# Second layer's slab built by DMAs inside SBUF instead of through a padded copy in DRAM

## The reference

```python
x = conv_same(x, w_init, b_init)                # 1x1: the "image"
offsets = conv_same(xi, w_off[g], b_off[g])     # 3x3, two numbers for each of 9 taps
sampled = sample_with_offsets(xi, offsets, K)   # bilinear, coordinates clipped to the image
h = depthwise_same(sampled, w_dw[g], b_dw[g])
outs.append(conv_same(h, w_pw[g], b_pw[g]))
```

## Time and profile before

| | |
|---|---|
| time, median of 3 runs | 294.44 us (291.98 to 295.67) |
| span of the profiled execution | 295.1 us |
| busy: PE / DVE / POOL / ACT | 79% / 66% / 47% / 19% |
| DMA | 5759 packets, 9.37 MB |

### The profile page before, as it was taken

How to read it: one execution, slowest core, us unless ns; L and a number is a source line. 1 busy time by engine, 2 the same in 40 slices (tenths; PEclk the granted TensorE clock), 3 DMA queues, 4 the chain that set the end, 5 groups by cost and what they waited for, 6 DMA issues and landing times.

```text
span 295.1 us, 2939 instructions
## 1 busy us (share of the span) xinstructions
PE 234.4 (79%) x908; PEld 134.6 (46%) x910; DVE 196.2 (66%) x476; ACT 57.0 (19%) x94; POOL 140.1 (47%) x196
## 2 busy tenths in 40 slices
PE   0959298988988789978883586889899788899990
PEld 0725096763336642224531142457578746343430
DVE  7767779979875387573309859998977144326286
ACT  1411924210001164513111000010101301310100
POOL 5300009786951509713404929999996010000560
PEclk9997969999996579999995769999999997799997
DMA  3529970000000000000166000000000000000000
GB/s 114 160 50 187 203 196 0 0 0 3 1 1 0 0 1 3 0 0 0 26 154 125 0 1 0 0 1 3 0 0 0 2 0 0 1 2 0 0 18 18
DMA packets 5759, 9.37 MB, mean 32 GB/s; under 512 B 2390, under 2 KB 2926, under 8 KB 5742
## 3 DMA queue, kind: packets, MB, share of 16 engines
q1 hardware_dynamic: 5742, 9.18, 13.3%
HBM read 7.48 MB, written 1.69 MB: 31 GB/s over the span
## 4 chain that ended last, share of the span: by engine, by line
PE 40%; DVE 30%; POOL 15%; issue 6%; ACT 5%; DMA 1%; DVEq 1%; POOLq 0%; ACTq 0%
POOL ring L265 12%; PE ps L1011 5%; PE ps L906 5%; PE ps L746 4%; PE ps L764 3%; DVE ps L1176 3%; PE ps L876 3%; DVE big L279 3%; PE ps L932 2%; DVE cm L1123 2%; DVE xn L1079 2%; PE ps L699 2%; PE ps L813 2%; DVE ring L287 2%; PE ps L727 2%
## 5 line engine op out<-in xcount | busy, mean ns | idle before, releaser
L265 POOL TENSOR_TENSOR ring<-big 128x384 f32<-128x384 f32 x72 | 59.2, 861 | 9.4 <-PE ps L906 4.6
L297 POOL TENSOR_TENSOR big<-big 128x512 f32<-128x512 f32 x30 | 32.0, 1095 | 38.6 <-ACT big L621 32.9
L906 PE MATMUL ps<-ring,ident 128*128 128x384 f32 x100 | 38.0, 523 | 10.2 <-POOL ring L265 5.7
L746 PE MATMUL ps<-ring,ident 128*128 128x192 f32 x126 | 26.4, 362 | 8.6 <-DVE ring L287 8.4
L1484 DVE TENSOR_TENSOR ps<-ps,ring 128x384 f32<-128x384 f32 x46 | 25.8, 562 | 9.6 <-PE ps L906 8.4
L906 PEld LDWEIGHTS ps<-ring,ident 128*128 128x128 f32 x100 | 19.1, 202 | 26.3 <-DVE ring L265 7.2
L746 PEld LDWEIGHTS ps<-ring,ident 128*128 128x128 f32 x126 | 22.6, 208 | 12.8 <-DVE ring L287 12.8
L433 POOL TENSOR_TENSOR rstd<-veps,mhalf 128x4 f32<-128x4 f32 x8 | 8.3, 1032 | 39.3 <-DVE veps L1075 39.2
L691 PE MATMUL ps<-zero,ident 128*128 128x512 f32 x34 | 22.7, 815 | 1.6 <-DVE big L1402 1.6
L554 POOL TENSOR_TENSOR big<-big 128x256 f32<-128x256 f32 (+1 forms) x12 | 7.6, 635 | 34.4 <-DVE big L1562 33.7
L265 DVE TENSOR_TENSOR ring<-big,ps 128x384 f32<-128x384 f32 x36 | 19.5, 546 | 0.1
(11 more groups left out here) (270 smaller groups left out, 397.5 us busy)
## 6 DMA issues: line engine op xcount, KB each, us to landing
big<-pad SPq DMA_DIRECT2D x8, 392.0 KB, 9.5
big<-pad SPq DMA_DIRECT2D x8, 240.0 KB, 5.5
w<-in_w_dram SPq DMA_DIRECT2D x2, 512.0 KB
w<-in_w_dram SPq DMA_DIRECT2D x2, 256.0 KB
pad<-img SPq DMA_DIRECT2D x8, 64.0 KB, 2.1
pad<-zero SPq DMA_DIRECT2D x1, 484.0 KB, 3.9
pad<-zero SPq DMA_DIRECT2D x1, 400.0 KB, 4.5
x<-in_x_dram SPq DMA_DIRECT2D x1, 256.0 KB, 2.6
```

The costliest lines, as they stand in the source:

```text
L265: return eng.tensor_tensor(V(ring, 0, slot * SP, [[1, P], [NJ * C, 3], [C1, NJ * G1], [1, C1]]), bigv((py + dy) * SLAB1 + (dx + j0) * C, [ ...
L297: return eng.tensor_tensor(dst, bigv(wy * SLAB0 + wx * C, [C0, J * G0], [1, C0]), table, ALU.mult)
L746: return mm(bank(px + dx, 0, P, [1, 3 * J * G0], off=dy * J * G0), ident[:, :], ring[:, slot + 3 * px * J * G0:slot + 3 * (px + 1) * J * G ...
L906: mm(bank(1 + i % 2, 0, P, [1, SP]), ident[:, :], ring[:, slot * SP:slot * SP + SP], start=(n == 0), stop=(n == len(srcs) - 1)).then_inc(s ...
```

## The change

The padded copy `pad1` goes, with its zero store at the start, its four stores and the eight slab loads. In their place:

- POOL clears the whole slab in `big` (3840 floats a partition) with one memset between `inv_std(5)` and `inv_std(6)`, once the semaphore `y0_ps` tells that PE has read what lies there (the hidden values of the experts).
- ACT copies the image from PSUM straight into the middle row of the slab instead of into `img`.
- SP issues two DMAs of 64 partitions x 512 bytes for the halo pixels, waits for both (`halo1`), and then four DMAs that copy the middle row (768 floats) of all partitions but the first or last few into the rows above (`slab1_above`) and below (`slab1_below`).
- POOL waits for the rows above ahead of its first product and for the rows below ahead of the second item. DVE waits for both at the place of the old wait.

```diff
-        pad0, pad1 = scratch("pad0", R0), scratch("pad1", R1)
+        pad0 = scratch("pad0", R0)
...
+            def window_rows():
+
+                mid = R1 * SLAB1
+                sp.wait_ge(sem("halo_zero"), 1)
+                sp.wait_ge(sem("img1"), 1)
+                for h, to, at in ((0, (R1 + HC) * C, R1 * C), (1, 0, HC * C)):
+                    sp.dma_start(V(big, h, mid + to, [[2, P // 2], [1, R1 * C]]),
+                                 V(big, 1 - h, mid + at, [[2, P // 2], [1, R1 * C]])).then_inc(sem("halo1"), 16)
+                sp.wait_ge(sem("halo1"), 32)
+                for wy, arrived in ((1, "slab1_above"), (0, "slab1_above"), (3, "slab1_below"), (4, "slab1_below")):
+                    shift = 2 * (wy - R1)
+                    n = P - abs(shift)
+                    sp.dma_start(V(big, max(0, -shift), wy * SLAB1, [[1, n], [1, SLAB1]]),
+                                 V(big, max(0, shift), mid, [[1, n], [1, SLAB1]])).then_inc(sem(arrived), 16)
...
-            sp.wait_ge(sem("img1"), 1)
-            image_out(pad1, R1, "img1", "pad1_stored")
-            slabs_in(pad1, R1, "pad1_stored", "slab1")
+            window_rows()
...
             inv_std(5)
+            pool.wait_ge(sem("y0_ps"), 1)
+            gp.memset(bigv(0, [1, N1 * SLAB1]), 0.0).then_inc(sem("halo_zero"), 1)
             inv_std(6)
...
-            pool.wait_ge(sem("slab1"), 128)
+            pool.wait_ge(sem("slab1_above"), 32)
             k = 0
             for i in range(N_ITEMS):
+                if i == 1:
+                    pool.wait_ge(sem("slab1_below"), 32)
...
-            sc.copy(V(img, 0, 0, [[1, P], [256, 2], [1, 256]]), bank(2, 0, P, [512, 2], [1, 256])).then_inc(sem("img1"), 1)
+            act.wait_ge(sem("halo_zero"), 1)
+            sc.copy(bigv(R1 * SLAB1 + R1 * C, [256, 2], [1, 256]), bank(2, 0, P, [512, 2], [1, 256])
+                    ).then_inc(sem("img1"), 1)
...
-                dve.wait_ge(sem("slab1"), 128)
+                dve.wait_ge(sem("slab1_above"), 32)
+                dve.wait_ge(sem("slab1_below"), 32)
```

More of the change, by code:

```diff
@@ L318, in _ @@
             sp.wait_ge(sem("zero_set"), 1)
-            for pad, reach in ((pad0, R0), (pad1, R1)):
-                n = B * (H + 2 * reach) * (W + 2 * reach) * C // P
-                sp.dma_start(V2(pad, [[n, P], [1, n]]), zero[:, 0:n]).then_inc(sem("pad_zeroed"), 16)
+            n = B * (H + 2 * R0) * (W + 2 * R0) * C // P
+            sp.dma_start(V2(pad0, [[n, P], [1, n]]), zero[:, 0:n]).then_inc(sem("pad_zeroed"), 16)
             load(w_out[:, :], "w_out", "w_o0")
@@ L373, in general_loads @@
                                  off=((b * (H + 2 * RB) + RB) * wd + RB) * C)
-                        sp.dma_start(dst, img[32 * b:32 * b + 32, :, :]).then_inc(sem(f"wide_img{tag}"), 16)
+                        src = (img[32 * b:32 * b + 32, :, :] if tag == 0 else
+                               V(big, 32 * b, R1 * SLAB1 + R1 * C, [[1, 32], [1, HC * C]]))
+                        sp.dma_start(dst, src).then_inc(sem(f"wide_img{tag}"), 16)
                     sp.wait_ge(sem(f"wide_img{tag}"), 16 * B)
@@ L385, in general_loads @@
                     sp.nop()
-            sp.wait_ge(sem("pad_zeroed"), 32)
+            sp.wait_ge(sem("pad_zeroed"), 16)
             image_out(pad0, R0, "img0", "pad0_stored")
```

## The result

The changed kernel takes 300.5 us (median of 4 runs, 299.8 to 301.1) against 293.7 us for the kernel before (4 runs side by side): ratio 1.022, interval 1.017 to 1.028. It is slower, by 5 to 8 us; whether by more than 2%, the interval leaves open.

The account below looks back on a forecast made before the run. No engine was taken as the bound throughout; the chain of waits decides. Median 294.44 plus 2.7 us for the memset holding DVE, 0 for slab and start, gave 297.1 us; range 293.2 to 300.8 for 8 in 10.

Parts of the forecast that it names:

- the rival in which the clock falls: After PE's 2.6 us pause behind L813 the clock halves, losing 1.7 to 3.0 us more: 298.8 to 300.1; chance 0.17.
- The likeliest case: Memset holds DVE, slab hidden, clock up: 297.1 us, own range 295.5 to 298.3; chance 0.51.
- DVE is held by the memset: End of layer 0's experts: a 3.23 us memset delays DVE's four L1079 by 2.7 us, all on the chain.
- The rival in which the memset is free: DVE's four L1079 get in ahead of the memset, so it costs nothing: 294.4 us; chance 0.15.
- the scaled row: An earlier memset beside L1079: DVE through 0.66 us after its end, less 0.13 for narrower instructions at the new place.
- The rule that was set beside it: DVE in two-port mode and a GpSimd instruction exclude each other throughout; DVE would lose 3.1 us, median 297.6.
- The clock stays up: From PE's pause behind L813 to the offset convolution the clock stays at 2.4 GHz, adding nothing.
- The slab costs nothing: Sampling stage: new slab arrives before it is needed, 0 us; cover 7.3 us for POOL's first product, 12.6 for DVE.
- as the rival had it: Rows below come late: 124-partition copies use four DMA engines, over 2% slower from 10.6 GB/s an engine down; chance 0.09.
- The bound of +0.6 us: Upper end of the slab's term: one more POOL collision lengthens a DVE weight product L279 by 0.64 us.
- A late slab helps: Sampling stage: POOL starting late lets DVE's L279 run at 0.45 us, gaining about 2 us: 295.1; chance 0.04.
- Nothing from an earlier slab and from the zero store: POOL's 0.1 us earlier start goes into its 4.20 us stall; nobody waits for the removed 400 KB store: 0 each.

Follow-up runs that it names:

- e3: The changed kernel plus two matmuls of zeros that fill PE's idle time while the memset holds DVE: 296.4 us, ratio 1.011.
- e1: The changed kernel with only the memset moved, from behind `inv_std(5)` to ahead of it: 296.5 us, ratio 1.008.
- e9: The kernel before, slab still through DRAM, plus the memset ahead of `inv_std(5)` and ACT's image copy waiting for it: 295.0 us, ratio 0.998.
- e2: The kernel before, slab still through DRAM, plus the memset between `inv_std(5)` and `inv_std(6)` and ACT's image copy waiting for it: 299.9 us, ratio 1.019.
- e5: e1 with the store of zeros into the second padded copy put back at the start: 296.8 us, ratio 1.006.
- e10: e1 with each row copy cut into 112 and 14 or 12 partitions: 296.4 us, ratio 1.006.
- e8_five_pairs: e1 with POOL's first product waiting for five of DVE's nine weight products instead of the first: 292.7 us, ratio 0.994.

## Why the prediction was right or wrong

The time, 300.5 us, lies inside the range, at its upper end, and 3.4 us above the forecast of 297.1. By ratio it is slower by 2.2% (1.7 to 2.8); the prediction gave 0.14 to slower by over 2%, and whether that is what happened the interval leaves open. The range holds the time only because its upper end was set by the rival in which the clock falls. The likeliest case had a range of its own, 295.5 to 298.3, and the time is outside it. (By its own terms the lower end should read 294.4 + 1.7 - 0.1 = 296.0.) Step by step:

- **DVE is held by the memset: right.** Forecast 2.7 us and a memset of 3.23 us; measured 2.56 us on DVE (3.54 against 0.98) and 3.30 us, in the traces; in the runs the hold alone was not resolved (e3 against e1). Which of the two starts first came out as in the trace of before, by the same 0.09 us. The rival in which the memset is free would have needed the other order, and e1 and e9 show that it is indeed free six microseconds earlier. The overhead behind the memset's end was 0.33 us and not the 0.53 that the scaled row gave. The rule that was set beside it (the Trainium skill, "SBUF — State Buffer", "SBUF: two separate sides") gives exclusion for the whole instruction; its direction agrees, and the size that the row gave was nearer. The run with twelve pieces shows more than either: 3.64 us for one DVE instruction across twelve POOL instructions.
- **The clock stays up: this is the step that failed.** It was priced as a rival, at 0.17, and it is what happened. The pause of PE came as computed (2.25 us against 2.6). The weight was too low: the row from 88 to 90 was read as a hint, although it was the nearest row to the question and showed PE with 0.77 of 2 us busy and the clock at 0.54 behind it. And its size was too small, 1.7 to 3.0 us where 3.60 were measured (e3 gives 3.7 back), though e2 shows that 1.6 us can come of the same pause. The length of the cold stretch was taken from one stretch at 22 to 25 us; here it lasted from 132.3 to 142.5. The trace of the kernel before had a better measure right behind the row from 88 to 90:

```profile
91.00:106.00 15.00, 13.20 (x49) 10.15 (x49) 7.99 (x38) 1.75 (x4) 5.19 (x12) 0.50 0.00 0
```

There PE had paused for 2.00 us, and the clock stood at 0.50 for 15 us with PE busy for 13.2 of them. Also the matmuls of zeros were counted as no work: at half the clock their 5.48 us came to lie on the chain.
- **The slab costs nothing: right on the chain, but the cover was overrated, and not quite right in the runs.** The estimates for the rows below were 156.9 for all engines and 160.2 to 169.3 for four; with the whole stage 4.3 us later, that is 161.2 and 164.5 to 173.6. They landed at 169.2. The rows above landed at 164.4 where 157.5 was computed, so the cover for POOL's first product was 0.5 us and not 7.3. The engines were four in the second part, as the rival had it, at 20 GB/s each in that part (16 from the first issue to the landing, by the prediction's own reckoning: 246 KB in 15.4 us), above the 12.3 at which it decides. The rule of the Trainium skill, "DMA: Bandwidth & Descriptors", "Why a DMA increments its semaphore by 16 and not by 1", of the largest divisor up to 16, agrees with the share of 0.25 behind the copies of 124 partitions; by the rate per engine that the prediction took from that page the rows would have been there at about 158, or 162 with the shift, and they came 7 us later. The bound of +0.6 us was too narrow against the 1.4 us that the runs show.
- **A late slab helps: right as a mechanism, and more than was said.** It was priced at 2 us of gain and 0.04, tied to transfers that are too slow. Made on purpose, by holding POOL and not the slab, it gives 2.6 us in the kernel before (means 294.9 to 292.3) and 3.6 over e1_memset_early (296.1 to 292.4). The working took POOL's order behind DVE as given, where one number of one wait changes it.
- **Nothing from an earlier slab and from the zero store: right for the chain** (from L896 to the end it is 150.7 us in both, and e5 stands with e1). But the slab came hardly earlier, so an early one was not tested by this kernel; e10, where the rows land well ahead, stands with e1.

The sum as measured: 2.56 for the hold, 3.60 for the clock, 1.83 less because the changed kernel's L1099 starts 1.83 us earlier than L1079 did, together the 4.3 us between the spans. The 1.83 us are no gain of the change: the profiled execution of the kernel before was 2.4 us over its median and that of the changed kernel 0.6. Between the means of the runs it is 4.3 us for the memset's place (300.5 over the 296.2 of e1, e5 and e10) and 1.4 us for the route, together the 5.7 us between 300.5 and the 294.8 of the 68 runs of the kernel before; the 6.8 us of the first comparison hold the scatter of its four runs.

## What to carry to other kernels

Before a long POOL memset or copy goes into a gap, look at what DVE runs beside it: here SBUF-to-SBUF work on DVE stood still for the whole of it, while DVE work that reads PSUM went on, so six microseconds earlier the same memset was free. Price a new pause of PE by the nearest row in which PE pauses and by the stage behind it at half the clock, matmuls that only keep the clock included, and consider filling the pause. Where two engines take turns on SBUF, try letting the one that others wait for finish first: one wait gave 0.9% here, where keeping the slab out of DRAM gave nothing and cost 0.5% as long as POOL started early.

## What was not expected of the hardware

- DVE did not get in between twelve back-to-back POOL memsets, one every 0.30 us; one DVE instruction of usually 0.30 us stood for 3.64 us.
- With DVE four products from its end, it was POOL that stood: its product took 2.02 us in place of 0.84 (e8_five_pairs).
- The clock stayed at 0.50 for some 10 us with PE busy for 8.93 of 9.00 us; with the same pause in e2_before_memset it was back at 1.00 after some 3.4 us. What decides between the two isn't known from these runs.
- Copies inside SBUF of 124 partitions ran at 80 GB/s; the same copies in 112 and 12 partitions at 240 to 253 GB/s.
- DVE products with both operands in SBUF take 0.45 us alone and 1.09 us where they alternate with POOL's products, and nine of them cost 3.4 or 7.9 us by the order alone.
